# One block number for each place instead of each pair, and the next chunk's scans ahead of this chunk's last additions

## The chip, the cores and the metric

One core of one Trainium2 chip. The metric is device microseconds of one execution; a kernel's time is the median of several.

## The reference

A graph of 3,125 nodes and 100,000 edges, sorted by destination, goes through two networks.

The first has four attention layers. In each, every edge gathers its source's key and value rows, and every node takes a softmax over the edges that come in:

```
alpha = sum(q[dst] * k[src]) / sqrt(16)          # 8 heads of 16
amax  = segment_max(alpha, dst)
ex    = exp(alpha - amax[dst])
out   = segment_sum(ex / segment_sum(ex, dst)[dst] * v[src], dst)
h     = layernorm(gated(out, h @ Ws) + h);  h = h + gelu(h @ W1) @ W2
```

The second is one pass of messages: silu(x[src] A + x[dst] B + rbf(length) C) summed over the destination, a mean, a small network and a layer norm. So there are five passes over all edges: four of attention and one of messages.

## The kernel before

**Places and chunks.** Nodes lie in 25 blocks of 128. Edges are laid out in places of 128; a place belongs to one block of destinations. Before the change places come in pairs of one block, so that 832 places (52 chunks of 16) are gathered in each pass. A chunk has four groups of four places. `slots` is a ring of four chunks.

**POOL** issues one indirect DMA for each place (line 432), 16 for a chunk: 128 rows of keys and values (1,056 bytes each) in attention, of 512 bytes in the messages. Before each group of four it waits for `slot_free[k][j]`, which PE raises when it has used up the group that lies in those slots. So POOL runs four chunks ahead of the use.

**The attention step of one chunk** (`attend_step` on DVE, PE and ACT), with n for the next chunk:

1. DVE: two scans of the transposed logits (lines 1124, 1126). PE turns four end columns into rows (712), ACT copies them (460, 463), DVE scans the carries along the chunk's heads (1135, 1140) and packs them (1146, 1151), PE turns them back (719, 720), ACT copies `icol` (469), and DVE scans again with the carries (1161, 1163). This gives each edge a running maximum of its node.
2. DVE: maximum and difference (1167, 1169). PE spreads the shift of the running maximum (728), ACT makes `scale` (474) and `ex` (477), PE turns `ex` (733), DVE weighs the values (1182), group by group.
3. PE adds a group up by one-hot matmuls (690, `add_up`), a pair of places in one region of bank 6 or 7, and DVE adds that to the block's row of `acc` (1092, `add_part`), eight additions for a chunk.
4. In between, for chunk n: ACT makes the turned one-hots (451) from PE's distances (667), PE spreads the queries (675, `rows`), DVE multiplies them into the keys (1102) and sums the heads (1108), and PE turns the logits (700, `turn_alpha`). DVE also makes chunk n's one-hots (1084), in two halves.

Each engine works in the order written. DVE does step 1 of chunk n only when all additions of the chunk before are done; PE does the groups in the order rows 1, rows 2, groups 0 and 1 up, rows 3, groups 2 and 3 up, and then turns the logits. The block numbers of a chunk's pairs are read into registers of PE and of DVE by one load of eight (line 283).

**The message step** has the same ring, the same `add_up` and `add_part`, but no scans: PE adds up groups 0 and 1, makes rows 0 and 1, then group 2, rows 2, group 3, rows 3; DVE makes messages (1199) and ACT takes their silu (517).

The lines that decide who waits for whom in `add_up` before the change:

```
pe.wait_ge(acc_done, START + (CH // 2) * g + max(2 * j - 2, 0))
for t in range(j * G, (j + 1) * G):
    o = (t % G) // 2 * HEADS * VW
    mm = pe.matmul(bank[6 + j % 2][:, o:o + width], oh[:, k % 2, t, :], slots[:, k, t, HID:HID + width],
                   start=(t % 2 == 0), stop=(t % 2 == 1))
mm.then_inc(slot_free[k][j], 1)
```

Of the kernel before, what the change touches and what calls it, by code (L numbers as in the profile page):

```python
# [25 lines left out]
L = 4  # L26
# [5 lines left out]
SUPERS = (-(-E // P) + NB - 1 + NB) // 2 + 1  # L32
CH = 16
RING = 4
CHUNKS = RING * (-(-2 * SUPERS // (RING * CH)))
V = CHUNKS * CH
VC = -(-V // P)
TURNS = CHUNKS // RING
# [20 lines left out]
assert NB % BW == 0 and V >= 2 * SUPERS  # L59


def build_program(nc, a, out):
    with ExitStack() as ctx:
# [22 lines left out]
        iota = sb("iota", [P, P])  # L86
        eps = sb("eps", [P, 1])
        count = bank[4][:, 3 * P:4 * P]
        place = sb("place", [P, 2, VC])
# [4 lines left out]
        ones = sb("ones", [P, P])  # L94
# [11 lines left out]
        super_blk = sb("super_blk", [1, VC * P // 2], I32)  # L106
# [16 lines left out]
        w_i = sb("w_i", [64, HID])  # L123
# [17 lines left out]
        f_out = sb("f_out", [1, HEADS, CH + 1])  # L141
        b_out = sb("b_out", [1, HEADS, CH + 1])
# [19 lines left out]
        def rows_of(n, width=P):  # L162
# [25 lines left out]
        den = sb("den", [P, BW, HEADS])  # L188
        rden = sb("rden", [P, BW, HEADS])
# [22 lines left out]
        blk = flat_slots[0:1, 10000:10000 + VC * P].bitcast(I32)  # L212
# [34 lines left out]
        slot_free = [sems(f"slot_free{k}_", NG) for k in range(RING)]  # L247
        oh_made, sq_spread, ohT_made, q_spread = sem("oh_made"), sem("sq_spread"), sem("ohT_made"), sem("q_spread")
# [8 lines left out]
        acc_scaled, acc_done = sem("acc_scaled"), sem("acc_done")  # L257
# [4 lines left out]
        counted = [sums_ready, deviations_ready, x_sums, x_devs, in_ps, in_act, s_ps, q_ev, h_ev, f2_ps, weighed, wo_ps, wo_ev, x_new, x_ps, x_out, src_ps, dst_ps, r_ps, pair_q, pair_s, a_ev, a_ps, acc_done, acc_scaled, acc_zero, act_ans, act_req,  # L262
# [4 lines left out]
                   max_done, node_done, ohT_made, oh_made, sq_spread, one_set,  # L267
# [3 lines left out]
                   *[s for ring in slot_free for s in ring]]  # L271

# [19 lines left out]
        def _(sp):  # L292
            sp.dma_start(su_i, a["dst_t"].rearrange("t e -> (t e)").rearrange("(p t) -> p t", p=P)).then_inc(ld_dst, 16)
            for dst, name in ((ident[:, :], "ident"), (iota[:, :], "iota"), (place[:, :, :], "place"),
# [17 lines left out]
            sp.dma_start(blk[:, :], flat_blk.rearrange("(a b) -> a b", a=1)).then_inc(su_prev, 16)  # L312
# [50 lines left out]
            def stage_layer(l):  # L363
                with sp.Fori(1, TURNS) as i:
                    for k in range(RING):
                        stage_indices(k, l, i)
# [27 lines left out]
            with sp.Fori(1, TURNS) as i:  # L394
                for k in range(RING):
                    stage_indices(k, L, i)
# [1134 lines left out]
```

## Time and profile before

| | |
|---|---|
| median of 3 runs | 8832.18 us (8828.31 to 8842.75) |
| the profiled execution | 8842.01 us |
| its span | 8840.1 us |
| mean granted TensorE clock | 0.663 of full speed |
| gathers in a pass of attention | 832, mean 0.951 us each |
| gathers in the pass of messages | 832, mean 0.947 us each |

Times in the rows below are microseconds from the start of the span unless they are marked ns. In a row of the timeline the first number is the start, the second the length, and the bracket holds the idle time of that engine before it and what ended it. "remote" stands for a wait whose end the profile can match to no engine. PE's starts are recorded and its ends are modelled. Register loads and branches are not counted as busy.

### The profile page before, as it was taken

Reading aid. Unit: us, or ns where it says so; the run is one execution under the profiler, and the core shown is the slowest. Engines: PE = TensorE matmul, PEld = TensorE weight load, DVE = VectorE, ACT = ScalarE, POOL = GpSimd, SP = SyncE. Lnnn points to the kernel's source line nnn. Section 1 sums busy time; section 2 is a strip of 40 time slices with the busy share of each in tenths; the row PEclk is TensorE's granted clock in tenths of the full one; section 3 lists DMA queues with packets and bytes.
Section 4 is the critical chain, followed back from the end, with each engine's and each line's share of the span. In section 5 each row is a group of like instructions: output and inputs, shape, how many; then the busy total and the mean of one; then the engine's idle time right before and its main releaser. Section 6 shows DMA issues by size and latency. Waiting matters only on the chain.

```text
span 8840.1 us, 92856 instructions
## 1 busy us (share of the span) xinstructions
PE 4798.1 (54%) x23521; PEld 3740.7 (42%) x23522; DVE 4034.4 (46%) x10004; ACT 1536.5 (17%) x2943; POOL 3970.3 (45%) x4185
## 2 busy tenths in 40 slices
PE   2455555564555555645555555555555555666667
PEld 1333444443444444434334444344433443555555
DVE  4444444453444444634444446444444454222223
ACT  0111111120111111211111111211111113333333
POOL 2444444414444444244444442344444433556552
PEclk9566666675666665766666666766666667877777
DMA  4222222222222222222222222222222221111111
GB/s 90 65 69 69 69 69 68 67 46 67 68 68 68 68 68 68 42 71 68 69 69 69 69 68 43 72 68 68 69 69 70 69 50 37 48 47 49 47 47 23
DMA packets 285864, 549.88 MB, mean 62 GB/s; under 512 B 132595, under 2 KB 164067, under 8 KB 285632
## 3 DMA queue, kind: packets, MB, share of 16 engines
q0 software_dynamic: 187040, 506.01, 22.5%
q1 hardware_dynamic: 91584, 35.25, 2.0%
q10 hardware_dynamic: 7072, 6.82, 0.2%
q8 instruction: 52, 0.85, 0.0%
q14 instruction: 116, 0.95, 0.0%
HBM read 527.86 MB, written 17.79 MB: 62 GB/s over the span
## 4 chain that ended last, share of the span: by engine, by line
another core or an unknown queue 44%; PE 21%; issue 19%; DVE 10%; ACT 3%; DVEq 1%; DMA 1%; ACTq 0%; SPq 0%; POOL 0%; POOLq 0%
PE bank L675 8%; PE bank L690 3%; PE bank L667 2%; DVE acc L1092 2%; PE bank L679 1%; PE bank L733 1%; PE bank L712 1%; DVE fwd L1161 1%; PE bank L831 1%; DVE bwd L1163 1%; ACT ex L477 1%; DVE oh L1084 1%; DVE slots L1199 1%; DVE alpha L1108 1%
## 5 line engine op out<-in xcount | busy, mean ns | idle before, releaser
L432 POOL DMA_INDIRECT slots<-kv_table,idx x3328 | 3162.4, 950 | 3995.5 <-PE bank L690 2441.8
L675 PE MATMUL bank<-qs,ohT 128*128 x8320 | 1916.3, 385 | 466.4 <-ACT ohT L451 163.1
L675 PEld LDWEIGHTS bank<-qs,ohT 128*128 128x128 f32 x8320 | 1628.4, 282 | 723.1 <-issue 701.4
L690 PE MATMUL bank<-slots,oh 128*128 128x136 f32 (+1 forms) x8320 | 1280.5, 308 | 173.2 <-issue 89.3
L690 PEld LDWEIGHTS bank<-slots,oh 128*128 128x128 f32 x8320 | 1192.5, 218 | 260.1 <-issue 140.5
L1092 DVE TENSOR_TENSOR acc<-acc,bank 128x136 f32 (+1 forms) x2080 | 606.3, 291 | 1353.5 <-remote 762.5
L432 POOL DMA_INDIRECT slots<-src_table,idx x832 | 787.7, 947 | 687.1 <-issue 243.3
L451 ACT ACTIVATE ohT<-bank,miss 128x512 f32<-128x512 f32 x1040 | 704.0, 682 | 959.7 <-PE bank L667 637.0
L1102 DVE TENSOR_TENSOR slots<-slots,bank 128x512 f32<-128x512 f32 x832 | 567.6, 682 | 330.7 <-remote 318.9
L719 PE MATMUL bank<-ones,c_row 1*128 1x1 f32 x416 | 119.8, 355 | 963.3 <-issue 696.3
L1084 DVE TENSOR_TENSOR oh<-bank,rel_e 128x1024 f32<-128x1024 f32 x520 | 629.5, 1212 | 0.1
L667 PE MATMUL bank<-terms,spread 12*128 12x512 bf16 x1040 | 572.8, 559 | 72.5 <-issue 67.7
L712 PE MATMUL bank<-ident,fwd 128*1 128x128 f32 x208 | 73.0, 351 | 929.4 <-issue 380.6
L1108 DVE TENSOR_REDUCE alpha<-slots 128x32 f32<-128x512 f32 x832 | 567.0, 681 | 0.5
L719 PEld LDWEIGHTS bank<-ones,c_row 1*128 1x128 f32 x416 | 102.1, 303 | 1065.2 <-issue 856.8
L1161 DVE TENSOR_TENSOR_SCAN fwd<-resets,icol,bank 128x128 f32<-128x128 f32 (+1 forms) x208 | 99.8, 480 | 979.3 <-ACT icol L469 966.4
L1182 DVE TENSOR_TENSOR slots<-slots,bank 128x544 f32<-128x544 f32 x832 | 541.8, 714 | 2.7 <-PE bank L733 2.7
L460 ACT COPY f_in<-bank 1x256 f32<-1x256 f32 x208 | 75.3, 362 | 2510.6 <-remote 1493.5
L1135 DVE TENSOR_TENSOR_SCAN f_out<-f_in 1x136 f32<-1x136 f32 x208 | 89.3, 429 | 835.4 <-issue 632.1
L1199 DVE TENSOR_TENSOR slots<-slots,bank 128x512 f32<-128x512 f32 x208 | 139.9, 684 | 626.9 <-remote 427.2
L712 PEld LDWEIGHTS bank<-ident,fwd 128*1 128x1 f32 x208 | 16.5, 79 | 967.0 <-issue 883.1
L679 PE MATMUL bank<-resets 128*128 128x128 f32 x1664 | 391.1, 322 | 31.0 <-issue 31.0
(242 smaller groups left out, 4407.2 us busy)
## 6 DMA issues: line engine op xcount, KB each, us to landing
slots<-kv_table,idx POOLq DMA_INDIRECT x3328
slots<-src_table,idx POOLq DMA_INDIRECT x832
kv_table<-slots SPq DMA_DIRECT2D x20, 660.0 KB, 3.7
resets<-flat_len ACTq DMA_DIRECT2D x52, 128.0 KB
idx<-src_e SPq DMA_DIRECT2D x260, 8.0 KB
terms<-flat_rel SPq DMA_DIRECT2D x260, 12.0 KB
w<-in_w SPq DMA_DIRECT2D x8, 256.0 KB
resets<-flat_rst SPq DMA_DIRECT2D x8, 208.0 KB, 10.1
```

Of the source, the lines that this page charges most:

```text
L432: pool.indirect_dma_start(slots[:, k, t, 0:width], None, table, bass.IndirectOffsetOnAxis(ap=idx[:, k, t:t + 1], axis=0))\
L451: act.activation(ohT[:, j % 2, :, :].rearrange("p a b -> p (a b)"), bank[j % 2][:, :], ACT.Relu, bias=miss[:, 0:1], scale=-1.0).then_inc(o ...
L667: pe.matmul(bank[j % 2][:, :], spread[:, j, :], terms[:, k, :], start=True, stop=True).then_inc(sq_spread, 1)
L675: mm = pe.matmul(o, ohT[:, j % 2, t, :], qs[:, blocks[(j * G + t) // 2], 0:HID], start=True, stop=basis is None)
L679: mm = pe.matmul(o, rbf[:, k % 2, half, :], m_1c[:, q, :], start=False, stop=True)
L690: mm = pe.matmul(bank[6 + j % 2][:, o:o + width], oh[:, k % 2, t, :], slots[:, k, t, HID:HID + width], start=(t % 2 == 0), stop=(t % 2 == 1))
L1084: dve.tensor_tensor(oh[:, k % 2, half * H:(half + 1) * H, :], bc(count[:, :], H), bcl(rel_e[:, bass.ds(c * CH + half * H, H)], P), ALU.is_ ...
L1092: dve.tensor_tensor(a_s, a_s, bank[6 + s // 2 % 2][:, o:o + width], ALU.add).then_inc(acc_done, 1)
L1102: dve.tensor_tensor(keys, keys, bank[2 + j % 2][:, :].rearrange("p (t k) -> p t k", t=G), ALU.mult).then_inc(spread_used, 1)
L1108: dve.tensor_reduce(alpha[:, :, j * G:(j + 1) * G].rearrange("p h t -> p t h"), slots[:, k, j * G:(j + 1) * G, 0:HID].rearrange("p t (h d) ...
L1182: dve.tensor_tensor(vals, vals, bcl(exs[:, j * G:(j + 1) * G, :], VW), ALU.mult).then_inc(w_done, 1)
L1199: dve.tensor_tensor(slots[:, k, j * G:(j + 1) * G, HID:2 * HID], slots[:, k, j * G:(j + 1) * G, 0:HID], bank[2 + j % 2][:, :].rearrange("p ...
```

## The change

Places no longer come in pairs. There are 806 of them (782 tiles of edges, and one more for each of 24 borders between blocks), in 51 chunks, the last with six places: `FULL` is 12 turns of the ring and `REM` is 3 chunks more. POOL gathers only places that exist. Each place has a block number of its own (`place_blk`), so that a chunk's load reads 16 numbers, and each place is added up by itself: a chunk's additions on DVE go from 8 to 16, each over one place. The results of `add_up` lie in six parts (3, 3, 3, 3, 2, 2 places) that alternate between banks 6 and 7. A part that doesn't end with a group raises a semaphore of its own, `part_ps`.

In attention the order changes too. DVE's `attend_step` now begins with the second scans; the first scans of chunk n stand after place 8's addition and the carry scans after place 11's, ahead of the additions of places 12 to 15. One copy packs both carries. The groups' weighing is spread between the additions. On PE, group 0 is added up before rows 2, and the turned logits and end columns of chunk n come before group 3. The one-hots of chunk n are made by ACT in attention: 16 activations |rel - count| and two of relu(1 - x).

```diff
+PLACES = -(-E // P) + NB - 1
+CHUNKS = -(-PLACES // CH)
+FULL, REM = CHUNKS // RING, CHUNKS % RING
+PARTS = ((0, 3), (3, 6), (6, 9), (9, 12), (12, 14), (14, 16))
+WITHIN = [m for m, (_, end) in enumerate(PARTS) if end % G]
...
-                super_blk[0:1, bass.ds(c * (CH // 2), CH // 2)], [engine], min_val=0, max_val=NB - 1,
+                place_blk[0:1, bass.ds(c * CH, CH)], [engine], min_val=0, max_val=NB - 1,
...
+            def onehots(l, g, k, prior):
+                act.wait_ge(acc_done, START + CH * (l * CHUNKS + prior))
+                for half in range(2):
+                    for t in range(half * CH // 2, (half + 1) * CH // 2):
+                        act.activation(oh[:, k % 2, t, :], iota[:, :], ACT.Abs, bias=rel_e[:, bass.ds((prior + 1) * CH + t, 1)],
+                                       scale=-1.0).then_inc(oh_far, 1)
+                    tiles = oh[:, k % 2, half * CH // 2:(half + 1) * CH // 2, :]
+                    act.wait_ge(oh_far, START + CH * (l * (CHUNKS - 1) + prior) + (half + 1) * CH // 2)
+                    act.activation(tiles, tiles, ACT.Relu, bias=1.0, scale=-1.0).then_inc(oh_made, 1)
...
-                pe.wait_ge(acc_done, START + (CH // 2) * g + max(2 * j - 2, 0))
                 for t in range(j * G, (j + 1) * G):
+                    part = next(m for m in range(len(PARTS)) if PARTS[m][0] <= t < PARTS[m][1])
+                    first, end = PARTS[part]
+                    if t == first:
+                        pe.wait_ge(acc_done, START + CH * g + (PARTS[part - 2][1] if part > 1 else PARTS[part - 2][1] - CH))
+                    o = (t - first) * HEADS * VW
+                    mm = pe.matmul(bank[6 + part % 2][:, o:o + width], oh[:, k % 2, t, :], slots[:, k, t, HID:HID + width],
+                                   start=True, stop=True)
+                    if t % G == G - 1:
+                        mm.then_inc(slot_free[k][j], 1)
+                    elif t == end - 1:
+                        mm.then_inc(part_ps, 1)
...
                 if ahead:
                     rows(n, kn, 1, blocks)
+                add_up(g, k, 0, HEADS * VW, w_done, g)
+                if ahead:
                     spread_terms(n, turn_n, kn, 3)
                     rows(n, kn, 2, blocks)
-                add_up(g, k, 0, HEADS * VW, w_done, g)
                 add_up(g, k, 1, HEADS * VW, w_done, g)
                 if ahead:
                     rows(n, kn, 3, blocks)
                 add_up(g, k, 2, HEADS * VW, w_done, g)
+                if ahead:
+                    turn_alpha(n)
+                    turn_ends(n)
                 add_up(g, k, 3, HEADS * VW, w_done, g)
-                if ahead:
-                    turn_alpha(n)
...
+                weigh(0)
+                if ahead:
+                    sum_heads(n, kn, 0)
+                weigh(1)
+                if ahead:
+                    multiply(n, l, i_n, kn, 1)
                 dve.wait_ge(acc_scaled, START + g + 1)
...
+                add(7, 8)
+                if ahead:
+                    first_scans(n, c + 1)
+                add(9, 10, 11)
+                if ahead:
+                    carries(n, c + 1)
+                add(12, 13, 14, 15)
```

In the message step DVE adds parts 0 and 1, waits for `slot_free[k][1]`, makes half the one-hots and messages 0 and 1, adds parts 2 and 3, makes messages 2, adds parts 4 and 5, and makes the rest; PE's order there stays as it was.

## Rows read from the trace of the kernel before

**Rows 1.** The page: span, and the chain that ended last, by engine.
```profile
span 8840.1 us, 92856 instructions
another core or an unknown queue 44%; PE 21%; issue 19%; DVE 10%; ACT 3%; DVEq 1%; DMA 1%; ACTq 0%; SPq 0%; POOL 0%; POOLq 0%
```

**Rows 2.** Windows: one attention layer, the messages; busy PE, PEld, DVE, ACT, POOL.
```profile
1967.00:3778.00 1811.00, 957.91 (x4470) 730.41 (x4470) 881.56 (x2238) 267.56 (x561) 791.16 (x832) 0.63 0.25 65
7395.00:8720.00 1325.00, 844.73 (x4986) 732.71 (x4986) 363.03 (x703) 413.53 (x603) 787.66 (x832) 0.78 0.20 47
```

**Rows 3.** Windows: 47 chunks of one attention layer.
```profile
2098.00:3600.00 1502.00, 780.07 (x3762) 609.05 (x3761) 724.74 (x1740) 196.65 (x434) 715.32 (x752) 0.62 0.26 68
```

**Rows 4.** Timeline of one chunk's period, all engines, 3055 to 3088.
```profile
3055.25 0.95 POOL L432 DMA_INDIRECT slots<-kv_table,idx  x1 [13.01 <-PE bank L690]
...
3056.46 2.02 PE L690 MATMUL bank<-slots,oh 128*128 128x136 f32 x16
...
3062.91 0.73 DVE L1092 TENSOR_TENSOR acc<-acc,bank 128x136 f32 x2 [4.03 <-remote]
...
3065.78 0.42 PE L712 MATMUL bank<-ident,rcol 128*1 128x128 f32 x1
...
3073.28 0.36 ACT L460 COPY f_in<-bank 1x256 f32<-1x256 f32 x1 [21.89 <-remote]
...
3074.03 0.95 POOL L432 DMA_INDIRECT slots<-kv_table,idx  x1 [0.30 <-issue]
...
3075.53 0.56 PE L720 MATMUL bank<-ones,c_row 1*128 1x1 f32 x2
...
3078.26 0.16 ACT L469 COPY icol<-bank 128x2 f32<-128x2 f32 x1 [0.72 <-remote]
...
3080.08 0.30 ACT L477 ACTIVATE ex<-bwd 128x128 f32<-128x128 f32 x1
...
3080.73 2.07 PE L675 MATMUL bank<-qs,ohT 128*128 x8
...
3085.13 2.32 PE L690 MATMUL bank<-slots,oh 128*128 128x136 f32 x16
...
3087.29 0.95 POOL L432 DMA_INDIRECT slots<-kv_table,idx  x1 [12.31 <-PE bank L690]
```

**Rows 5.** Timeline of ACT in the period that began at 2545.
```profile
2554.28 0.16 ACT L469 COPY icol<-bank 128x2 f32<-128x2 f32 x1 [1.23 <-issue]
...
2568.57 0.18 ACT L474 ACTIVATE scale<-bank 128x8 f32<-128x8 f32 x1 [12.10 <-remote]
```

**Rows 6.** Timeline of DVE at a layer's last chunks, with no gathers.
```profile
3634.72 0.41 DVE L1124 TENSOR_TENSOR_SCAN fwd<-resets,bank 128x128 f32<-128x128 bf16 x1
...
3672.47 0.41 DVE L1124 TENSOR_TENSOR_SCAN fwd<-resets,bank 128x128 f32<-128x128 bf16 x1
```

**Rows 7.** Timeline of POOL in the messages: first gather behind the ring's first fill, a stop, the last.
```profile
7489.02 1.70 POOL L432 DMA_INDIRECT slots<-src_table,idx  x1 [13.95 <-DMA idx<-src_e]
...
7862.66 0.95 POOL L432 DMA_INDIRECT slots<-src_table,idx  x1 [0.30 <-issue]
7866.45 0.95 POOL L432 DMA_INDIRECT slots<-src_table,idx  x1 [2.85 <-remote]
...
8698.01 0.94 POOL L432 DMA_INDIRECT slots<-src_table,idx  x1 [0.30 <-issue]
```

**Rows 8.** Line 283: the load of a chunk's block numbers; min/median/max ns.
```profile
L283 DVEq TENSOR_LOAD <-super_blk x260: 594/598/864, 268.4 to 8747.0; - x130
```

**Rows 9.** Groups by line, whole span: busy us, mean ns, idle before.
```profile
L1084 DVE TENSOR_TENSOR oh<-bank,rel_e 128x1024 f32<-128x1024 f32 x520 | 629.5, 1212 | 0.1
L1092 DVE TENSOR_TENSOR acc<-acc,bank 128x136 f32 (+1 forms) x2080 | 606.3, 291 | 1353.5 <-remote 762.5 <-PE bank L690 466.5 <-issue 44.2
...
L477 ACT ACTIVATE ex<-bwd 128x128 f32<-128x128 f32 x208 | 64.4, 310 | 97.0 <-DVE bwd L1169 96.9
L460 ACT ACT_TABLE_LOAD x48 | 61.6, 1283 | 795.4 <-remote 413.4 <-issue 247.8 <-PE bank L712 134.2
```

More of the change, by code:

```diff
@@ L363, in stage_layer @@
             def stage_layer(l):
-                with sp.Fori(1, TURNS) as i:
+                with sp.Fori(1, FULL) as i:
                     for k in range(RING):
                         stage_indices(k, l, i)
+                for k in range(REM):
+                    stage_indices(k, l, FULL)
             load_keys(0)
@@ L393, in _ @@
                              kvst[:, i * BW:(i + 1) * BW, 0:HID]).then_inc(tab_out, 16)
-            with sp.Fori(1, TURNS) as i:
+            with sp.Fori(1, FULL) as i:
                 for k in range(RING):
                     stage_indices(k, L, i)
+            for k in range(REM):
+                stage_indices(k, L, FULL)
             for i in range(NI - 1):
@@ L422, in _, with gather_chunk @@
                     pool.reg_mov(uses[k][j], 0)
-            def gather_chunk(k, turn, l, table, width):
+            def gather_chunk(k, turn, l, table, width, places=CH):
                 used = [pool.snap(uses[k][j]) for j in range(NG)]
@@ L428, in gather_chunk @@
                 for j in range(NG):
-                    pool.wait_ge(slot_free[k][j], START + used[j])
-                    pool.reg_add(uses[k][j], uses[k][j], 1)
-                    for t in range(j * G, (j + 1) * G):
+                    if isinstance(turn, int):
+                        pool.wait_ge(slot_free[k][j], START + turn)
+                    else:
+                        pool.wait_ge(slot_free[k][j], START + used[j])
+                        pool.reg_add(uses[k][j], uses[k][j], 1)
+                    for t in range(j * G, min((j + 1) * G, places)):
                         pool.indirect_dma_start(slots[:, k, t, 0:width], None, table,
@@ L620, in _ @@
             turned_onehots(L * CHUNKS, 1)
-            with act.Fori(0, TURNS - 1) as i:
+            with act.Fori(0, FULL) as i:
                 for k in range(RING):
                     message_step(i, k, True)
-            for k in range(RING):
-                message_step(TURNS - 1, k, k < RING - 1)
+            for k in range(REM):
+                message_step(FULL, k, k < REM - 1)
             def means_turned(i):
@@ L778, in _ @@
             pe.wait_ge(su_count, 1)
-            pe.matmul(bank[7][:, 0:NB + 1], ones[:, :], row[:, 0, :], start=True, stop=True).then_inc(su_count, 1)
+            pe.matmul(bank[7][:, 0:NB + 1], all_ones, row[:, 0, :], start=True, stop=True).then_inc(su_count, 1)
             pe.wait_ge(ld_const, 16 * 15)
@@ L1185, in attend_step, with add @@
-                for j in range(1, NG):
-                    if ahead:
-                        multiply(n, turn_n, kn, j)
-                    add_part(g, turn, k, 2 * j - 2, blocks, HEADS * VW)
-                    if ahead:
-                        sum_heads(n, kn, j)
-                    add_part(g, turn, k, 2 * j - 1, blocks, HEADS * VW)
-                for s in (CH // 2 - 2, CH // 2 - 1):
-                    add_part(g, turn, k, s, blocks, HEADS * VW)
-            def messages(g, turn, k, j):
-                dve.wait_ge(kv_in[k][j], 16 * G * (turn + 1))
+                def add(*places):
+                    for t in places:
+                        add_place(g, turn, k, t, blocks, HEADS * VW)
@@ L1198, in messages @@
+            def messages(g, i, k, j):
+                dve.wait_ge(kv_in[k][j], landed(L, i, k, j))
                 dve.wait_ge(q_spread, START + NG * g + j + 1)
```

247 lines of the change are left out of this document (140 added, 107 removed).

## The prediction

> **What bounds the kernel now.** The page gives PE 21% of the chain that ended last, DVE 10%, and 44% to "another core or an unknown queue", on one core with no other at work [rows 1]. So the time is neither PE's nor DVE's work, and the next view is the windows: an attention layer takes 1811 us with PE busy 958, DVE 882, POOL 791 [rows 2]. Inside it, 47 chunks take 1502.0 us, 31.96 each, for 16 gathers [rows 3]. There are 48 such periods in a layer (52 chunks less the ring's four), 192 in all: 6136 of 8840 us. They are what the change works on.
>
> The timeline of one period shows where its 32 us go [rows 4]. I call the first gather's start 0 (3055.25).
> - POOL issues 16 gathers, the last at 18.8, one in 1.25 us, and then waits 12.3 us for PE's group 0: the ring is full, so POOL doesn't set the pace; whoever frees group 0 does.
> - PE's signals arrive late while POOL gathers. PE's last group is drawn as ended at 3058.48, and DVE's additions that wait for it start at 3062.91, 4.4 late. The end columns are turned at 3066.20, and ACT copies them at 3073.28, 7.1 late. The carries are turned at 3076.09, ACT copies them at 3078.26, which is 4.2 us after the last gather's start (23.0).
> - From then on nothing is late: ex at 24.8, rows 1 at 25.5, group 0 up at 29.9, the next burst at 32.0.
>
> Even where the chain is lucky and `icol` is there at 9.0, `scale` comes only at 23.3 after the burst's start [rows 5]. So at least one of PE's signals is held in each period until about 4.2 us behind the last gather, and a period is 23 us of burst and drain and 9 us of chain behind it. Without gathers a chunk takes 18.9 us (37.75 for two) [rows 6]: the engines' own chain, hidden nowhere.
>
> The Trainium skill (Perfetto Trace Analysis, Tensor Engine Instruction) says that a matmul's drawn end is an estimate, and that its signal goes out when PSUM has acknowledged the writes; why the acknowledgement waits for gathers it doesn't say, and the trace agrees that drawn end and signal differ by up to 7 us.
>
> **Fewer chunks.** In each attention layer one whole period goes (32.0), and the last burst has 6 gathers in place of 16. Those ten are 12.5 us of issue; the engines' own chain then shows (18.9 and some drain, say 22), so I take 10. 4 x (32.0 + 10.0) = 168 us less. Bounds: 128 (nothing for the short burst) and 180.
>
> **The new order, one period.** I take the same zero, and the gathers at the same rate.
> - PE adds up group 0 right behind rows 1, which end at 3082.80, in place of 3085.13 [rows 4]: the next burst starts 2.3 us sooner after `ex`. Before, ex to next burst was 3080.08 to 3087.29, 7.2; now 4.9.
> - The price: rows 2, rows 3 and their signals now fall into the burst. Rows 3 are ready at about 3.4, like the signal that was 4.4 us late at 3.2. So DVE multiplies group 3 at 7.7; with addition and head sums (0.7, 0.3, 0.7) the logits are turned at 9.6 instead of 3.7. That signal is held like the one raised at 10.9 (7 us) or less: 14 to 17. First scans and turned ends: 2 us, 16 to 19.
> - Group 3 is added up behind the turned ends, so its slots come free only then. POOL wants them for gather 13, at 15.0. It stops, and its stop drains the queue: in the messages POOL goes on 3.8 us after its last gather's start [rows 7], in attention all was through 4.2 after it [rows 4]. The twelfth starts at 13.8, so all that was raised arrives at about 17.6, and POOL goes on at about 18.1.
> - Copies, carry scans and the turn back took 2.8 us (3073.28 to 3076.09): `icol` at 20.3. DVE has four additions (0.37 each when in a run, from 0.73 for two) and then the load of 16 numbers, twice 0.598 [rows 8], before the second scans: about 22.0, where it was 23.2.
> - The shift is spread at about 23, in the second burst of four (18.1 to 21.9 for the last start), and is held until 21.9 + 4.2 = 26.1. Then ex, and 4.9 us more: 31.0.
>
> So the period goes from 31.96 to 31.0, and 46 periods in each of four layers give 184 x 0.96 = 177 us less. Both sides are wide: 28.3 if no signal is held early, 34.2 if one more is (rivals).
>
> **What I cost at nothing.** DVE's one-hots go (two of 1.21) and eight additions of 0.291 come [rows 9]: 2.4 for 2.3. ACT gets 16 activations of 128x128 (nearest row: 0.31) and two of 1024 columns (twice 0.69 each): 7.7 us behind the turned one-hots of group 3, done near 9; the copies behind them in ACT's queue wait for 14 or more anyway. With that cover gone, as in the last four chunks, ACT has 4.2 + 7.7 of 18.9 us. No Abs is in the trace; a table of its own would add two loads of 1.28 [rows 9], still covered. The longer load of block numbers is covered on DVE by the held shift (22.0 + 1.6 + 2.5 of slack); without that it costs 184 x 1.2 = 220 us, on PE it lies in idle time. The setup loses some ten small instructions, under 2 us.
>
> The Trainium skill (Runtime: NRT & Kernel Launch, Instruction fetch mechanics) gives some 200 ns for each register loaded, which would be 3.2 us for 16 where the row says 0.598 us for eight; the second scans would then start at 24.0 and nearly use up the slack, and the slow rival would be likelier. The row is of this very load, so I go by it.
>
> **The messages.** 48 chunks take 1210 us, 25.2 each [rows 7]. One fewer and a short one: 25 + 12.5 = 38 less. But PE's places 6 and 7 now wait for DVE's additions 0 to 2, and group 3 for additions 6 to 11; before, the additions it waited for were long done. That is two more trips PE to DVE and back in a chunk, between nothing and two held signals (0 to 8 us). POOL is the faster side there too, but only by 5 us in 25, so I take 2.0: 47 x 2.0 = 94 more. Sum +56, bounds -38 and +338.
>
> **Sum.** 8842.0 (the profiled execution, 1.9 over its span) - 168 - 177 + 56 = 8553. The median of the runs is 10 less than that execution: 8545.
>
> **Rivals.**
> - *One signal more is held (slower).* If the turned logits arrive only with POOL's stop at 17.6, scans and ends take until 19.5, group 3 is up at 20.5, POOL goes on at 21.2, and its last four gathers drain at 21.2 + 3.8 + 4.2 = 29.2; with 4.9 that is 34.2. In all periods: 184 x 2.24 = +412, with -168 + 56 some 9135. It decides from a mean of 32.6 us, that is when it holds for half of the periods. For it: the 7.1 us of the third held signal [rows 4]. Against: it must be held 8 us from 9.6. Chance 0.25.
> - *The early signals get through.* As in [rows 5], the chain is then done to `icol` by 10, group 3 is free before 15, POOL doesn't stop, scale comes at 23.3 and the next burst at 28.3: 184 x -3.66 = -673. With -168 and -38, some 7955. For it: the first 3 us of a burst hold nothing. Against: group 3's queries are raised at 3.4, and a signal raised at 3.2 was already 4.4 us late. Chance 0.15.
> - *The order changes nothing.* The earlier start of the burst is paid back by the later signals, the period stays 31.96, and only 168 + 38 go: 8625. Chance 0.15.
>
> My forecast, a mixture of 30 to 32 us with the messages a little longer, has 0.45. Its own range is 8380 to 8740.
>
> **Range and chances.** I leave out the lower half of the fast rival and the upper part of the slow one: 8200 to 8960. Faster by over 0.2% (18 us, about what a measurement tells from no change): 0.45 + 0.15 + 0.15 less the upper edges of these, 0.68. Slower: most of the slow rival, and a mixture with long messages, 0.26. Between: 0.06.
>
> **What the profile would show.** Right: POOL's bursts fall into twelve and four, the stop ending some 4 us behind the twelfth gather; the second scans near 22; `scale` waits for a held signal near 26; bursts 31 us apart; message chunks near 27. Wrong, if bursts stay whole at 16, if DVE's load of 16 takes over 2 us or stands on the path, if ACT's one-hots delay line 460, or if the messages' chunks reach 30.

## The result and the profile after

The changed kernel takes 8173.1 us (median of 4 runs, 8158.2 to 8175.5), the kernel before 8830.9 beside it: a ratio of 0.925 (95% interval 0.923 to 0.927), 7.5% faster. The forecast was 8545 us, 3.2% faster, and the time lies below the range of 8200 to 8960. A second comparison, after_same below, gave 0.923 (0.922 to 0.925).

The page after, its span and chain; before stands in [rows 1].

```profile
span 8173.0 us, 107094 instructions
PE 27%; another core or an unknown queue 23%; issue 22%; DVE 16%; ACT 6%; DVEq 4%; ACTq 1%; DMA 0%; SPq 0%; POOL 0%; POOLq 0%
```

The share of unknown releasers fell from 44% to 23% of the span, 3890 us to 1880. That is the wait that no engine's record explains; what stands behind it follows below.

Windows: one attention layer, 45 of its chunks, the messages up to their tail. They answer to [rows 2, 3].

```profile
1810.80:3442.50 1631.70, 917.12 (x4390) 726.49 (x4390) 876.41 (x2458) 596.41 (x1452) 765.40 (x807) 0.66 0.26 71
1939.60:3237.50 1297.90, 724.00 (x3604) 592.20 (x3603) 701.35 (x1890) 488.47 (x1227) 683.86 (x720) 0.65 0.29 76
6695.40:8040.00 1344.60, 842.88 (x4842) 719.45 (x4842) 465.75 (x1060) 402.39 (x584) 761.07 (x806) 0.79 0.17 45
```

A layer went from 1811 to 1631.7 us. Its period is now 1297.9 / 45 = 28.84 us, where it was 31.96 and the forecast said 31.0. Less work doesn't explain it: DVE is busy 15.6 us of a period (701.35 / 45), before 15.4 (724.74 / 47), ACT 10.9 for 4.2, and PE 16.1 for 16.6, which is 0.5 of the 3.1 us.

The timeline of one period after, which answers to [rows 4]; I count from 3010.51.

```profile
3010.51 0.95 POOL L458 DMA_INDIRECT slots<-kv_table,idx  x1 [7.32 <-PE bank L737]
...
3012.47 1.05 PE L719 MATMUL bank<-qs,ohT 128*128 x8
...
3014.40 0.96 PE L737 MATMUL bank<-slots,oh 128*128 128x136 f32 x6 [0.64 <-issue]
...
3019.27 0.95 POOL L458 DMA_INDIRECT slots<-kv_table,idx  x1 [0.30 <-issue]
3022.02 0.69 DVE L1163 TENSOR_TENSOR slots<-slots,bank 128x512 f32<-128x512 f32 x1 [7.67 <-remote]
...
3022.87 0.94 POOL L458 DMA_INDIRECT slots<-kv_table,idx  x1 [2.66 <-remote]
...
3025.66 0.42 PE L758 MATMUL bank<-ident,rcol 128*1 128x128 f32 x1
...
3026.12 0.36 ACT L503 COPY f_in<-bank 1x256 f32<-1x256 f32 x1 [8.28 <-PE bank L758]
...
3029.76 0.15 ACT L512 COPY icol<-bank 128x2 f32<-128x2 f32 x1
...
3029.80 0.94 POOL L458 DMA_INDIRECT slots<-kv_table,idx  x1 [2.10 <-PE bank L737]
...
3031.04 0.48 DVE L1219 TENSOR_TENSOR_SCAN fwd<-resets,icol,bank 128x128 f32<-128x128 f32 x1 [1.05 <-issue]
...
3031.32 0.18 ACT L517 ACTIVATE scale<-bank 128x8 f32<-128x8 f32 x1 [0.81 <-PE bank L780]
...
3032.65 0.31 ACT L520 ACTIVATE ex<-bwd 128x128 f32<-128x128 f32 x1 [1.16 <-DVE bwd L1227]
...
3033.55 0.95 POOL L458 DMA_INDIRECT slots<-kv_table,idx  x1 [0.30 <-issue]
...
3037.97 0.95 POOL L458 DMA_INDIRECT slots<-kv_table,idx  x1 [3.47 <-PE bank L737]
```

What is to be seen:
- The burst is broken twice: eight gathers, a stop to 12.4, four, a stop to 19.3, four; the next burst starts at 27.5. The forecast had one stop, behind the twelfth. Of the 180 full periods (45 in each of four layers) 174 have the first stop and 159 the second.
- PE has added up group 2 at 4.9 (3015.36, line 737), long before POOL wants its slots at 10.0. POOL still waits for it, until 12.4, and the view names no engine. The trace also records when each semaphore was raised. This one was raised at 3022.11, 6.8 us behind the drawn end of the matmul that raises it; rows 3's at 3022.00, 8.5 us behind. So POOL waits for a signal of PE that comes late while POOL's own gathers run.
- Rows 3 are ready at 3.0, and DVE multiplies group 3 at 11.5, in the same stop: 2.75 us behind the eighth gather's start. From here no signal is more than 1.1 us late: end columns turned at 15.6 and copied at once, where before they were copied 7.1 late; `icol` at 19.3, `scale` at 20.8 and not at the 26.1 of the forecast, `ex` at 22.1. In the mean of the 180 periods `scale` starts at 22.1 and `ex` at 23.6, and the next burst 5.3 us after `ex`. Before, these were 24.0, 24.6 and 7.3.

Groups of line and engine, whole span: DVE's multiplication, ACT's `f_in` and `scale`.

```profile
L1163 DVE TENSOR_TENSOR slots<-slots,bank 128x512 f32<-128x512 f32 x816 | 558.3, 684 | 1311.9 <-remote 1288.0 <-issue 20.2 <-PE bank L719 1.9
L503 ACT COPY f_in<-bank 1x256 f32<-1x256 f32 x204 | 73.6, 361 | 1141.8 <-issue 732.8 <-PE bank L758 378.1 <-remote 30.1
L517 ACT ACTIVATE scale<-bank 128x8 f32<-128x8 f32 x204 | 36.2, 177 | 356.1 <-PE bank L780 133.9 <-remote 120.7 <-issue 101.5
```

DVE still waits for the queries behind a held signal, 1288 us or 6.3 a chunk, in the period above that of rows 3. `f_in`'s wait for one is gone (30 us), and `scale`'s is down to 0.6 us a chunk.

The semaphore events show the hold by themselves, and that it is PE's alone. I take the time from the drawn end of the last instruction that raises a semaphore to the recorded raise. In the window of [rows 3], 261 of PE's 760 recorded raises come over 1 us late, the latest by 11.9 us; of the 1467 by DVE and ACT none is over 0.02 us late. In the 45 chunks of the changed kernel it is 223 of 784, and again none of DVE's and ACT's. So the signals are still held after the change, but fewer of those that the chain to `ex` waits for.

### The profile page after: what moved, and what is told of

Same layout as the page of the kernel before. It is cut to its first block, busy times and chain, and to the rows that moved or that the text cites. A ratio compares the mean times of both kernels' runs of the same rounds, so it can differ in the third digit from the quotient of the medians.

```text
span 8173.0 us, 107094 instructions
## 1 busy us (share of the span) xinstructions
PE 4670.9 (57%) x23101; PEld 3738.2 (46%) x23102; DVE 4125.0 (50%) x11274; ACT 2847.6 (35%) x6495; POOL 3842.8 (47%) x4055
## 4 chain that ended last, share of the span: by engine, by line
PE 27%; another core or an unknown queue 23%; issue 22%; DVE 16%; ACT 6%; DVEq 4%; ACTq 1%; DMA 0%; SPq 0%; POOL 0%; POOLq 0%
PE bank L719 9%; PE bank L737 7%; DVE acc L1148 6%; ACT oh L491 3%; PE bank L711 2%; DVEq L302 2%; PE bank L723 2%; PE bank L758 1%; DVE alpha L1169 1%; PE bank L785 1%; DVEq L1148 1%; PE bank L885 1%; DVE oh L1135 1%; DVE slots L1238 1%
## 5 line engine op out<-in xcount | busy, mean ns | idle before, releaser
L458 POOL DMA_INDIRECT slots<-kv_table,idx x3224 | 3061.6, 950 | 3382.7 <-PE bank L737 1370.2
L737 PE MATMUL bank<-slots,oh 128*128 128x136 f32 (+1 forms) x8160 | 1613.6, 351 | 578.2 <-DVE acc L1148 502.6
L719 PE MATMUL bank<-qs,ohT 128*128 x8160 | 1689.4, 354 | 220.3 <-ACT ohT L483 119.1
L737 PEld LDWEIGHTS bank<-slots,oh 128*128 128x128 f32 x8160 | 1427.3, 252 | 715.5 <-DVE acc L1148 624.1
L719 PEld LDWEIGHTS bank<-qs,ohT 128*128 128x128 f32 x8160 | 1437.0, 255 | 440.5 <-issue 418.2
L1148 DVE TENSOR_TENSOR acc<-acc,bank 128x136 f32 (+1 forms) x4080 | 1189.2, 291 | 628.5 <-PE bank L737 161.9
L491 ACT ACTIVATE oh<-iota,rel_e 128x128 f32<-128x128 f32 x3200 | 972.6, 388 | 0.0
L561 ACT ACTIVATE slots<-slots 128x512 f32<-128x512 f32 x204 | 128.5, 630 | 948.3 <-DVE slots L1282 822.1
L495 ACT ACTIVATE oh<-oh 128x1024 f32<-128x1024 f32 x400 | 422.6, 1057 | 12.6
L723 PEld LDWEIGHTS bank<-resets 128*128 128x128 f32 x1632 | 319.7, 242 | 12.4 <-issue 12.0
```

Of the source, the lines that this page charges most:

```text
L458: pool.indirect_dma_start(slots[:, k, t, 0:width], None, table, bass.IndirectOffsetOnAxis(ap=idx[:, k, t:t + 1], axis=0))\
L491: act.activation(oh[:, k % 2, t, :], iota[:, :], ACT.Abs, bias=rel_e[:, bass.ds((prior + 1) * CH + t, 1)], scale=-1.0).then_inc(oh_far, 1)
L495: act.activation(tiles, tiles, ACT.Relu, bias=1.0, scale=-1.0).then_inc(oh_made, 1)
L719: mm = pe.matmul(o, ohT[:, j % 2, t, :], qs[:, blocks[j * G + t], 0:HID], start=True, stop=basis is None)
L723: mm = pe.matmul(o, rbf[:, k % 2, half, :], m_1c[:, q, :], start=False, stop=True)
L737: mm = pe.matmul(bank[6 + part % 2][:, o:o + width], oh[:, k % 2, t, :], slots[:, k, t, HID:HID + width], start=True, stop=True)
```

## The experiments

Two theories: **A**, the gain is that POOL's burst is broken, and in its stops PE's held signals get through. **B**, the gain is the order's own; the stops only go with it. The period of each run is one window from the fifth chunk's first gather in the second layer, divided by its chunks, as above. The kernel before ran again beside each set of runs. Where it takes 8741 to 8848 us, it differs by some 0.5 us a period from set to set, so a smaller difference between periods of different sets says nothing.

### Stops in the kernel before, and none in the changed kernel

```diff
 # b_land23; b_land2 has (2,)
                 for j in range(NG):
+                    if table is kv_table and j in (2, 3):
+                        pool.wait_ge(kv_in[k][j - 1], 16 * G * (turn + 1))
                     pool.wait_ge(slot_free[k][j], START + used[j])
 # a_whole
+                if table is kv_table:
+                    pool.wait_ge(slot_free[k][NG - 1], START + (turn if isinstance(turn, int) else used[NG - 1]))
```

> The kernel before, in which POOL in attention also waits, ahead of groups 2 and 3 of each chunk, until the group before them has landed: the burst of 16 gathers becomes 8 + 4 + 4 and nothing else changes. Theory A (the changed kernel is fast because POOL's burst is broken and PE's held signals get through in the pauses): the period of 31.96 us goes towards the 28.8 of the changed kernel, 192 x -3.2 = some -600, so about 8230 us, and DVE's and ACT's waits of 7 us behind PE's results shrink to 4. Rival B (the gain is the new order's, the pauses only accompany it): the last gather comes some 5 us later and with it the release of the last held signal, so the period goes to 33 to 37 us, 9030 to 9800 us.

> The kernel before with one such wait only, ahead of group 2: the burst becomes 8 + 8. Theory A: part of the gain, a period of about 30 to 31.5 us, 8450 to 8740 us. Rival B: 2 to 3 us more a period, 9200 to 9400 us. If 8 + 8 is slower and 8 + 4 + 4 faster, what counts is how few gathers run behind the last pause.

> The changed kernel, in which POOL in attention starts a chunk's gathers only when group 3's slots are free as well, so that all 16 go in one burst without a stop. The ring is still more than two chunks ahead. Theory A: signals raised in the burst are held for up to 23 us again, and the period goes from 28.8 to 32 us or more: 184 x 3.2 = +590 or more, 8760 us and up. Rival B (the order alone makes the gain): POOL has 13 us to spare in a period and nothing is late, the time stays within 1% of 8173 us.

Measured: b_land23 7660 us, a ratio of 0.877 (0.874 to 0.880); b_land2 7658, 0.876 (0.874 to 0.878); a_whole 8739, 0.999 (0.998 to 1.000). The kernel before took 8749 there. Windows of b_land23 (47 chunks), b_land2 (47) and a_whole (45):

```profile
1757.38:2989.33 1231.95, 748.73 (x3655) 594.26 (x3656) 710.69 (x1693) 190.85 (x425) 712.07 (x752) 0.65 0.31 83
```
```profile
1767.30:2991.06 1223.76, 773.91 (x3778) 612.51 (x3776) 732.03 (x1742) 193.58 (x434) 712.36 (x752) 0.66 0.31 84
```
```profile
2081.18:3537.09 1455.91, 769.31 (x3601) 636.85 (x3600) 700.85 (x1890) 488.41 (x1226) 683.90 (x720) 0.66 0.25 68
```

Waiting more makes the old kernel 12% faster: 26.2 and 26.0 us a period for 31.96 (5.7 us a period by the kernels' times, 1091 / 192). B expected 33 to 37. A's direction is right, and its size too small: the period went below the changed kernel's 28.8. A period of b_land23, POOL and ACT:

```profile
2202.07 0.95 POOL L434 DMA_INDIRECT slots<-kv_table,idx  x1 [2.64 <-issue]
...
2205.39 0.36 ACT L462 COPY f_in<-bank 1x256 f32<-1x256 f32 x1 [21.12 <-PE bank L714]
...
2208.01 0.16 ACT L471 COPY icol<-bank 128x2 f32<-128x2 f32 x1 [1.32 <-issue]
...
2210.12 0.94 POOL L434 DMA_INDIRECT slots<-kv_table,idx  x1 [2.73 <-DMA slots<-kv_table,idx]
...
2210.69 0.18 ACT L476 ACTIVATE scale<-bank 128x8 f32<-128x8 f32 x1 [1.54 <-PE bank L730]
```

The whole chain from `f_in` to `scale` takes 5.3 us there, around the second stop. And the new order with whole bursts is back at 32.35 us. One caution: a_whole not only joins the burst, it also starts it later, so its 3.5 us are the two together; b_land2 and b_land23 only add waits.

### The old order with the single places

In a_old_order PE and DVE have in attention the order of before (the diff of the change, taken back: group 0 behind rows 2, all weighing ahead of the additions, scans and carries last), with 806 places, six parts and ACT's one-hots kept.

> The changed kernel with the order of before in attention: PE adds up group 0 behind rows 2 and turns the next chunk's logits and end columns behind group 3; DVE weighs all groups at once and makes its first scans and carry scans behind all additions. The 806 single places, the six parts and ACT's one-hots stay. By the prediction's terms the order is worth 177 us at most and this comes to some 8350 us, if the places' share was under-sized. If the order makes the gain (through the broken burst or by itself), the period is 32 us again: 8173 + 184 x 3.2 = 8760 us; if single places and ACT's one-hots alone broke the burst, it stays at 8173 us.

Measured: 9126 us, 1.044 (1.041 to 1.047). 45 chunks:

```profile
2157.60:3687.42 1529.82, 785.75 (x3600) 609.88 (x3600) 709.36 (x1891) 493.01 (x1225) 680.77 (x720) 0.62 0.24 65
```

34.0 us a period: none of the expected values. With the old order, single places, six parts and ACT's one-hots together cost some 2.0 us a period, which outweighs the fewer chunks. I had costed them at nothing in attention. The order is worth all of 34.0 - 28.8 = 5.2 us. The burst isn't whole here: in 162 of 180 periods POOL stops ahead of group 3, 2.1 us in the mean, and in only 2 ahead of group 2. That is the burst of twelve and four that the forecast had for the changed kernel, and `scale` comes at 26.0 in the mean, where the forecast has 26.1. So a stop behind the twelfth gather alone brings no gain here.

### The parts of the order, and the size of a gather

```diff
 # a_g0_late: PE
                     rows(n, kn, 1, blocks)
-                add_up(g, k, 0, HEADS * VW, w_done, g)
                 if ahead:
                     spread_terms(n, turn_n, kn, 3)
                     rows(n, kn, 2, blocks)
+                add_up(g, k, 0, HEADS * VW, w_done, g)
 # a_scans_late: PE, and DVE likewise
+                add_up(g, k, 3, HEADS * VW, w_done, g)
                 if ahead:
                     turn_alpha(n)
                     turn_ends(n)
-                add_up(g, k, 3, HEADS * VW, w_done, g)
 # b_narrow, from the kernel before
+                        width, table = (64, a["x"]) if table is kv_table else (width, table)
                         pool.indirect_dma_start(slots[:, k, t, 0:width], None, table,
```

> The kernel before, in which each gather of the attention passes fetches 128 rows of 64 numbers (256 bytes) of another table in place of 264 (1,056 bytes); the keys and values are left out, and once a layer the unused columns are set to zero (some 13 us a layer). As many gathers, a quarter of the bytes. If bytes in flight hold PE's signals, the signals get through within a burst, scale no longer waits until 4 us behind the last gather, and the period falls to between 20 (16 gathers of 1.25 us) and 26 us: 6500 to 7650 us. If gathers as such hold them, however small, the period stays at 31 to 32 us and the time at 8650 to 8800 us.

> The changed kernel, with PE's group 0 added up behind rows 2 as before; all else stays. The prediction has the earlier group 0 at 2.3 us a period (184 x 2.3 = 423): some 8600 us. If only the break of the burst counts, and the burst still breaks ahead of groups 2 and 3, the time stays within 1% of 8173 us.

> The changed kernel, with the first scans and carry scans of the next chunk behind all additions on DVE, and turned logits and end columns behind group 3 on PE; group 0 stays early. Group 3's slots then come free some 3 us sooner, without waiting for the turned logits. Theory A: POOL stops less ahead of group 3, its last eight gathers run as one burst, and scale is held: 30 to 34 us a period, 8400 to 9100 us. Rival B: only the scans' place counts, their 2 to 3 us come back on the chain, and the burst is broken as now: 8550 to 8700 us, with POOL's stop ahead of group 3 unchanged at 2.8 us. If neither matters: 8173 us.

> The changed kernel with the explicit waits of b_land23: POOL in attention goes on with groups 2 and 3 only when the group before has landed. Theory A: the burst is already broken at these places in 9 of 10 periods, so little changes, 8050 to 8200 us. If it is the depth of POOL's lead that still costs (queries and messages late), it goes towards the 26.1 us a period of b_land23: 8173 - 184 x 2.7 = 7680 us. If the stops only add to the burst: 8300 us and up.

The last of them is the changed kernel with the stops of b_land23 (its diff stands two parts below). These four ran on a chip where the kernel before takes 5972.6 us, not 8750 to 8850. Measured: b_narrow 5969 us, 0.999 (0.998 to 1.000); a_g0_late 6232, 1.044 (1.042 to 1.046); a_scans_late 6453, 1.080 (1.078 to 1.082); a_land23 6846, 1.146 (1.144 to 1.148). So I ran three of them again together with the changed kernel itself:

> The changed kernel itself, unaltered, beside the kernel before on the same chip. The last four kernels ran on a chip on which the kernel before takes 5973 us with POOL at 1.25 us a gather throughout, not 8750: there no signal of PE is held. Theory A (the gain is that held signals get out): where the kernel before takes 8750 to 8830 us, the ratio is 0.92 to 0.93; where it takes 5973 us, POOL sets the pace at 20.0 us a chunk in both, only the 26 gathers fewer a pass count (5 x 26 x 1.25 = 163 us), and the ratio is 0.97 at best. Rival B (the order shortens the chain itself): the ratio is 0.92 to 0.93 on either.

> The changed kernel with PE's group 0 behind rows 2 again, once more, for a chip that holds signals. Where the kernel before takes 8750 to 8830 us: the prediction's 2.3 us a period make 1.052 times the changed kernel; if only the break of the burst counts, it is within 1% of it. Where the kernel before takes 5973 us: 6232 us as before.

> The changed kernel with the scans of the next chunk behind all additions, once more, for a chip that holds signals. Where the kernel before takes 8750 to 8830 us, theory A: the burst is no longer broken ahead of group 3, a period of 30 to 34 us, 8400 to 9100 us; rival B: 8550 to 8700 us with the burst broken as now. Where the kernel before takes 5973 us: 6453 us as before.

> The kernel before with gathers of 256 bytes a row in place of 1,056, once more, for a chip that holds signals. If bytes in flight hold them, the time falls to 6000 to 7650 us, as on the other chip or nearly; if gathers as such hold them, it stays at 8650 to 8800 us. Where the kernel before takes 5973 us: 5969 us as before.

This time the kernel before took 8848 us. Measured: after_same 8169 us, 0.923 (0.922 to 0.925); a_g0_late_2 8631, 0.975 (0.974 to 0.977); a_scans_late_2 8777, 0.991 (0.990 to 0.993); b_narrow_2 8918, 1.008 (1.007 to 1.010).

The same kernel, b_narrow, on either chip: a window of 47 chunks, POOL's gathers, ACT's `icol`. First the chip of 5973 us:

```profile
1406.92:2347.81 940.89, 768.87 (x3867) 617.79 (x3867) 744.59 (x1784) 202.17 (x446) 711.76 (x752) 0.70 0.14 27
```
```profile
L434 POOL DMA_INDIRECT slots<-in_x,idx x3328 | 3147.6, 946 | 1471.0 <-issue 1469.8 <-PE bank L692 1.2
L471 ACT COPY icol<-bank 128x2 f32<-128x2 f32 x208 | 33.3, 160 | 236.9 <-PE bank L722 236.9
```

and the chip of 8848 us:

```profile
2130.56:3641.88 1511.32, 785.47 (x3760) 614.02 (x3759) 724.72 (x1740) 196.72 (x434) 712.68 (x752) 0.62 0.09 17
```
```profile
L434 POOL DMA_INDIRECT slots<-in_x,idx x3328 | 3155.3, 948 | 4078.6 <-PE bank L692 2529.8 <-issue 1509.4 <-remote 39.3
L471 ACT COPY icol<-bank 128x2 f32<-128x2 f32 x208 | 33.4, 160 | 888.3 <-remote 834.6 <-PE bank L722 39.0 <-issue 14.7
```

Three things follow.
- Whether signals are held differs with the chip that a set of runs had. On the first every wait of `icol` ends with PE's record, and POOL issues a gather each 1.25 us without a stop (20.0 us a chunk); none of PE's 821 recorded raises in the window is over 0.02 us late. On the second 835 of 888 us end with nothing the profile knows, and 266 of 747 raises are over 1 us late. I call the chips holding and free from here on. The five later sets of runs had five chips, each one only once, so whether this is the chip's own or was so for that time alone isn't shown.
- Bytes don't matter: with 256 of 1,056 bytes a row, and DMA engines 9% busy for 26%, a holding chip still needs 32.2 us a period. The number of gathers and of rows is the same in both, and which of these counts isn't shown.
- On the holding chip group 0's early place is worth 31.15 - 28.8 = 2.3 us and the scans' 32.0 - 28.8 = 3.2 us. Windows of a_g0_late_2 and a_scans_late_2:

```profile
2043.20:3444.89 1401.69, 750.13 (x3600) 607.38 (x3600) 695.81 (x1892) 489.75 (x1229) 683.15 (x720) 0.66 0.26 70
```
```profile
2076.30:3516.85 1440.55, 783.89 (x3602) 606.27 (x3602) 708.91 (x1891) 493.95 (x1227) 682.23 (x720) 0.62 0.26 69
```

The first looks like the forecast's own 2.3 us, but that is in part luck. From `ex` to the next burst it is 7.2 us in the mean there and 5.3 in the changed kernel, so the early place is worth 2.0 us; the other 0.3 lie ahead of `ex`, and POOL's second stop is there in only 50 of 180 periods, not 159. In the second, POOL of a_scans_late_2 shows the stop that is left, ahead of group 2, and then eight gathers in one go:

```profile
2307.19 0.94 POOL L458 DMA_INDIRECT slots<-kv_table,idx  x1 [0.30 <-issue]
2310.82 0.94 POOL L458 DMA_INDIRECT slots<-kv_table,idx  x1 [2.69 <-remote]
...
2319.57 0.95 POOL L458 DMA_INDIRECT slots<-kv_table,idx  x1 [0.30 <-issue]
...
2333.54 0.94 POOL L458 DMA_INDIRECT slots<-kv_table,idx  x1 [13.03 <-PE bank L737]
```

A's picture, in A's range: of 180 periods 173 have the first stop and 7 the second. With the scans ahead of it, group 3 is late enough for the second stop; bringing that about is part of what their move does.

### Explicit stops in the changed kernel, single places, one-hots

```diff
 # a_land23; a_old_land23 and a_old_land2 are a_old_order with it, the last with (2,)
                 for j in range(NG):
+                    if table is kv_table and j in (2, 3):
+                        pool.wait_ge(kv_in[k][j - 1], landed(l, i, k, j - 1))
 # a_oh_dve: ACT's onehots(l, g + 1, ...) goes, and on DVE behind arg_done
+                if ahead:
+                    for half in range(2):
+                        H = CH // 2
+                        dve.tensor_tensor(oh[:, kn % 2, half * H:(half + 1) * H, :], bc(iota[:, :], H),
+                                          bcl(rel_e[:, bass.ds((c + 1) * CH + half * H, H)], P), ALU.is_equal).then_inc(oh_made, 1)
```

> The changed kernel with explicit stops ahead of groups 2 and 3, once more, for a chip that holds signals. Where the kernel before takes 8750 to 8850 us: if POOL's natural stops (all periods ahead of group 2, 8 of 10 ahead of group 3) already give all there is, 8050 to 8200 us; if a stop that always ends only with the landing lets more through, towards POOL's own 25.0 us a period, as this kernel has it where nothing is held: 8173 - 184 x 3.8 = 7470 us. Where the kernel before takes 5973 us: 6846 us as before.

> The changed kernel's 806 single places with the old order and explicit stops ahead of groups 2 and 3. If the order is worth nothing once the burst is broken, it equals a_land23_2 within 1%. By its unbroken twins (34.1 against 32.0 us a period) single places cost the old order 2.1 us: 26.1 + 2.1 = 28.2 us a period and some 8060 us. If single places cost only through signals held in a whole burst: 26.1 us a period, 7660 - 5 x 26 = 7530 us. Where nothing is held: 6846 us or a little more.

> The same with one stop, ahead of group 2. With pairs of places one stop was worth as much as two (7658 and 7660 us), so within 1% of a_old_land23 on a chip that holds signals. If single places need the second stop, 200 to 500 us more. Where nothing is held, POOL's pace of 22.5 us a chunk: 6300 to 6450 us.

> The changed kernel with the next chunk's one-hots on DVE, in two halves of 1.2 us between DVE's difference and its wait for scale, not on ACT. The prediction costs ACT's one-hots at nothing, and DVE waits for scale or ex there in most periods: within 1% of the changed kernel (ratio 0.92 to 0.93) where signals are held. If DVE's time counts fully: 184 x 2.4 = +440 us, 8610 us. Where nothing is held: the kernel is on POOL's pace or just off it, 5850 to 6250 us.

On a holding chip (the kernel before took 8741 us): a_land23_2 7728, 0.884 (0.882 to 0.885); a_old_land23 7985, 0.913 (0.911 to 0.915); a_old_land2 8282, 0.948 (0.946 to 0.950); a_oh_dve 8295, 0.948 (0.947 to 0.950). Windows of a_land23_2 and a_old_land23, 45 chunks each:

```profile
1804.16:3033.64 1229.48, 713.37 (x3489) 585.00 (x3490) 681.70 (x1841) 474.43 (x1186) 682.84 (x720) 0.64 0.30 80
```
```profile
1878.35:3160.45 1282.10, 770.07 (x3537) 597.78 (x3536) 697.96 (x1853) 485.79 (x1208) 682.63 (x720) 0.65 0.29 77
```

- 27.3 against 28.5 us: with the stops in both, the order itself is worth 1.2 of its 5.2 us. The other four go with the stops that it brings about.
- Stops that always come (27.3) beat the natural ones (28.8), which are missing ahead of group 3 in about one period of nine (21 of 180). Those 21 periods take 29.8 us and the others 28.7.
- Single places, with the parts and ACT's one-hots, cost 2.3 us where both kernels have both stops (28.5 against b_land23's 26.2).
- One stop is enough with pairs (26.0) and not with single places (30.1 against 28.5). I had expected them equal. Against a_old_order's 34.0, with its natural stop behind the twelfth gather, the stop behind the eighth is worth 3.9 us.
- With the one-hots on DVE a period takes 1.0 us more (29.8), and the kernel 2.5%: not the nothing that I had, and not the full 2.4. This isn't DVE's time alone: POOL's stop ahead of group 3 is there in only 28 of 180 periods. A period of the changed kernel without that stop takes 29.8 us too, but in a_oh_dve itself the 28 periods with the stop are no shorter than the rest (29.9 and 29.6). So how much is the lost stop and how much DVE's time stays open.

### The order with pairs of places

b_early is the kernel before with the changed kernel's order on PE and DVE, in pairs, and both one-hot halves on DVE where a_oh_dve has them.

> The kernel before (832 places in pairs, 52 chunks, one-hots on DVE) with the changed kernel's order: group 0 added up early, first scans, carry scans, turned logits and ends ahead of the last additions. Both halves of the one-hots stand between DVE's difference and its wait for scale. Where the kernel before takes 8750 to 8850 us: if the order with its natural stops is what gains, and single places are a burden (2.1 us a period in the old order), 27 to 29 us a period, 7850 to 8250 us; if the single places with their longer additions are what makes POOL stop, the burst stays whole and the period is 31 to 32 us, 8650 to 8850 us. Where it takes 5973 us: POOL's 20.0 us a chunk, 5970 us, or up to 22 us, 6350 us.

> The same with explicit stops ahead of groups 2 and 3. If the order adds to the stops, POOL's own pace of 25.0 us a chunk: 7450 to 7550 us, below the 7660 of b_land23. If the stops are all and the order nothing: 7660 us within 1%. If the order is a burden once the stops are there: 7800 us and up. Where nothing is held: POOL's 25.0 us a chunk, some 6930 us.

The second run had b_early's kernel again by mistake, without stops: it is a second reading of the same kernel and tests nothing of its expectation. Both ran on a free chip (the kernel before took 5971 us): 6081 and 6078 us, 1.018 (1.017 to 1.020) both times. On a free chip the order, with the one-hots in their new place, costs 1.8%. What order and stops give together with pairs on a holding chip wasn't tried.

## Why the prediction was wrong, point by point

- **What bounds the kernel.** Right on the chips that hold: PE's signals are held while gathers run, and set the pace. The semaphore events show the hold (261 of 760 raises), and b_land2 and b_land23 that it sets the pace, since they only add waits.
- **Fewer chunks, -168.** The four periods are there (4 x 32 = 128). The short last burst gave nothing, where I took 10 a layer: from the last chunk's first gather to the next pass's first, the second layer takes 177.8 us now and 178.3 before.
- **The period, 31.0 us: the step that failed.** "POOL wants them for gather 13": I took it that only group 3's slots would be late, so that POOL stops only behind the twelfth gather, and that the shift is then held until 26.1. But group 2's slots, which PE frees at 4.9 in the new order, are late as well. I had 4.4 us of lateness for a signal raised at 3.2; that would have given 9.3, just ahead of the 10.0 at which POOL wants them. The trace has 6.8 us for it, and 8.5 for rows 3, where I had 4.3. POOL finds nothing at gather 9 and stops there, in 174 of 180 periods. By 12 the held signals are through, not by 17.6; the end columns, which the forecast has raised and held between 14 and 19, are copied at once; and the last four gathers, which I had holding the shift, mostly don't. `scale` comes at 22.1 in the mean and not at 26.1; `ex` follows 1.5 later and the next burst 5.3 after that, where the forecast had 0 and 4.9. That is 28.84 for 31.0, 184 x 2.2 = 400 us more than forecast, and the only large miss. Where the burst does fall into twelve and four, in a_old_order, `scale` comes at 26.0. The forecast knew that a stop drains the queue, and priced a stop only as something that comes; it never asked what a stop behind the eighth gather would give. b_land2 is the answer: 5.7 us a period. Why a signal raised at 3 to 5 is held until the stop now, and one raised at 3.2 had passed by 7.7 in the period of [rows 4], is open.
- **ex to the next burst, 4.9.** 5.3 in the period shown and in the mean, for 7.3 before and 7.2 in a_g0_late_2. Right, 2.0 us for the 2.3.
- **What was costed at nothing.** Wrong in three places that the larger gain hid: single places some 2.0 to 2.3 us a period (perhaps because PE's parts wait for DVE's additions of held parts, 503 us ahead of line 737 in the whole span, before 74; no run tests the reason); ACT's one-hots up to 1.0 in the change's favour, by DVE's time or through POOL's second stop; and the load of 16 block numbers. The last is no longer covered, since the shift is no longer held: DVE's second scans wait 1.7 us a chunk for nothing but issue (348.7 us over 204), near what I had put on it "without that" (1.2). `ex` now starts 1.5 us behind `scale` in the mean, before 0.7. The group, and the load:

```profile
L1219 DVE TENSOR_TENSOR_SCAN fwd<-resets,icol,bank 128x128 f32<-128x128 f32 (+1 forms) x204 | 97.9, 480 | 369.2 <-issue 348.7 <-ACT icol L512 20.5
```
```profile
L302 DVEq TENSOR_LOAD <-place_blk x255: 1096/1101/1358, 285.8 to 8075.4; - x128
```

The load takes 1.10 us for 16 registers, against 0.598 for eight [rows 8]. The Trainium skill (Runtime: NRT & Kernel Launch, Instruction fetch mechanics) has some 200 ns a register for such a load, which would be 3.2 us. The page gives that price among the launch's own loads, and this load reads SBUF. The trace has 69 ns a register, and the trace decides.

- **The messages, +56.** Measured +33 with the tail (1477.6 us from the pass's first gather to the end of the span, before 1444.8). A chunk takes 26.6 us and took 25.3: 1.3 more where I took 2.0 for the parts' extra trips.
- **The rivals.** "Early signals get through" was nearest in its period (28.3), but for another reason: it had whole bursts and no stop. "One more is held" had POOL stopping as a price only. Neither had the stop as the gain.

The sum against the trace: -128 for the periods fewer, 184 x -3.12 = -574 for the shorter ones, +33 for the messages, +11 for the setup (first gather at 181.0, before 169.6) and some -9 for the layers' first and last chunks: -667, and the spans differ by 667.1.

**The best version seen** is b_land2 (b_land23 is its equal): the kernel before and one wait, 7658 us on a holding chip, a ratio of 0.876 against 0.925 for the change. On a free chip such stops only cost: a_land23 has 25.0 us a chunk there, which is POOL's 20.0 and two stops, and is 14.6% slower than the kernel before.

## What to carry to other kernels

When waits end on a releaser that the profile can't name, ask what runs meanwhile on an engine that has time to spare, and try a stop there before reordering the engines that wait: one wait on POOL gave 12%, a rewritten order 7.5%. Price a new stall by what it lets through as well as by its length, and follow each signal the change moves into a burst, the ones that free the burst's own slots too. Compare on several chips: here the sign of an edit hung on which one it ran on. And look at what else an edit moves: group 0's place and the one-hots' engine each changed how often POOL stopped.

## What was unexpected of the hardware

- While POOL's indirect gathers follow each other at 1.25 us, PE's signals can be held: 8.5 us for rows 3 in the period shown, up to 11.9 us in the window of the kernel before. DVE's and ACT's are not (none of 1467 over 0.02 us). Some pass within a burst (before 7.7 in [rows 4]); the rest come through about 2.8 us after the eighth gather's start, where POOL stops there, and 4.2 after the sixteenth's. Rows of 256 bytes hold them as rows of 1,056 do.
- The chips differ: the kernel before took 8831 us in the first comparison and 8741 to 8848 us in three more sets of runs, but 5971 and 5973 us in two others; the last five had five different chips. On the free ones none of it is seen: in a_g0_late's window none of PE's 894 recorded raises is over 0.02 us late, and in the same kernel on a holding chip 270 of 863 are over 1 us late. What makes a chip hold is open, as is by which path a gather delays PE's signal. The changed kernel itself never fell on a free chip; its nearest relatives there, a_g0_late and b_early, were 4.4% and 1.8% slower than the kernel before. So that the change is a gain there is not shown.
